# All 32 row moves of both routed layers issued one behind another, ahead of the first put

## The chip, the cores and the metric

One core of one Trainium2 chip. The metric is the time of one execution on the device in microseconds. The kernel runs a whole small network in one launch.

## The reference

Four blocks of cross-attention and feed-forward on x (4 x 512 tokens, 128 features), each with a layer norm before it and a residual add. Blocks 1 and 4 have a routed feed-forward ("layer 0" and "layer 1" in this text): each token goes to the two best of eight experts, and its results are summed with the gates. Cut to that:

```
x = x + xattn0(ln(x), ctx)
x = x + ffn0(ln(x))     # gates = softmax(x @ gate_w); top 2 of 8 experts; gelu(x @ fc[e]) @ proj[e]
x = x + xattn1(...); x = x + ffn1(...)      # dense over experts
x = x + xattn2(...); x = x + ffn2(...)
x = x + xattn3(ln(x), ctx)
x = x + ffn3(ln(x))     # top 2 of 8; (silu(x @ wg[e]) * (x @ wu[e])) @ down[e]
```

The routed layers compute only the chosen pairs of token and expert, and so does the kernel: 2048 tokens x 2 choices = 4096 rows, sorted by expert.

## The kernel before

The 2048 tokens are 16 tiles of 128. A routed layer goes through these steps:

- DVE and PE work out for each token and choice the row that it gets in a buffer in HBM, `xw` (`slot_i`), first for tiles 0 to 7, then for tiles 8 to 15. The semaphore `routed` counts the halves.
- POOL copies rows into `xw` by 32 indirect DMAs, called **moves** (`scatter`, L678 to L684): one for each tile and choice, 128 rows of 130 numbers each. They come in seven groups: tiles 0 to 4 (10 moves), 5 (2), 6 (2), 7 (2), 8 and 9 (4), 10 and 11 (4), 12 to 15 (8), from the table `MOVED` (L37). Each group counts its landings on one of four semaphores `scattered`, so group n first waits for group n - 4.
- `xw` is then read in 39 **slots** of 128 rows, each of one expert. SP loads a slot's rows into one of four buffers `xrow` (L487), as soon as the groups that it needs have landed (`FILLED`: slots 0 to 2 need group 0, slot 3 group 1, 5 group 2, 7 group 3, 9 group 4, 13 group 5, 17 group 6).
- For slot t PE transposes the rows (L2399), ACT copies the result into `xT` (L888, semaphore `ex_xc`), and PE multiplies with the up weights (L2411: 8 matmuls of 128x128 in layer 0, 16 in layer 1), which DVE has copied to `wcur` (L1440, once the up-projection four slots earlier has freed a buffer: semaphore `ex_up`). ACT applies the activation (L893, waits on `ex_up` too), in layer 1 DVE multiplies (L1455), and PE multiplies with the down weights (L2422, 8 matmuls, semaphore `ex_dn`). ACT copies the result into one of eight buffers `Y` (L904; in layer 0 every other turn of eight goes to a second set, `attn`).
- POOL writes each slot's result to its tokens' places in HBM, `yt`, by an indirect DMA, called a **put** (`put`, L686 to L700), once ACT has made it. SP loads `yt` back by pieces and DVE adds it to X.

All engines run their own program in the order written, and meet by semaphores. What sets the order of moves and puts on POOL is its function `experts(layer)` (L706 to L735) alone. Three things in it matter here:

- `BURSTS` (L38): in layer 0 groups 1, 4 and 6 wait until the group before them has landed; in layer 1 group 1 does.
- `pause()` (L702 to L704): a memset of 128x192 numbers that POOL itself then waits for. The buffer is used by nothing at that time. It stands behind each of the first 24 puts of both layers, and in layer 1 also ahead of each move from group 3 on.
- In layer 1 group 3 also waits for ACT's first copy of the layer (`ex_xc`), and the eight moves of the last group stand between the first four puts, two behind each.

Of the kernel before, what the change touches and what calls it, by code (L numbers as in the profile page):

```python
# [20 lines left out]
TILES = B * S // P  # L21
# [4 lines left out]
E, TOPK = 8, 2  # L26
# [7 lines left out]
SLOTS = (TILES * P * TOPK + PARTIAL) // P  # L34


MOVED = (0, 5, 6, 7, 8, 10, 12, TILES)  # L37
BURSTS = ((1, 4, 6), (1,))  # L38
FILLED = [-(-(tiles * P * TOPK - PARTIAL) // P) for tiles in MOVED[1:-1]]

FIRST_DONE = (GT * P * TOPK * 3 // 2 + PARTIAL) // P
# [7 lines left out]
RING = 4  # L49
# [72 lines left out]
def build(nc, p0, p1, p3, cols, rows, bias, x, mask0, mask3, fc0, pj0, fc1, pj1, fc3, pj3,  # L122
          wkv, wq2, wout2, w1t, w2t, cw, out):
    ctx = ExitStack()
    with ctx:
# [3 lines left out]
        def sem(name):  # L129
            return ctx.enter_context(nc.semaphore(name))  # L130
# [189 lines left out]
        with nc.sbuf_tensor("XHL", [P, GROUPS, 2, 2, S], F32R) as XHL:  # L320
# [55 lines left out]
        scattered = [sem(f"scattered{i}") for i in range(4)]  # L376
        table_ready, table_mm = (sem(n) for n in ("table_ready", "table_mm"))
        x_loaded = [sem(f"x_loaded{i}") for i in range(RING)]
        ex_t, ex_xc, ex_w, ex_up, ex_act, ex_dn, ex_y = (
            sem(n) for n in ("ex_t", "ex_xc", "ex_w", "ex_up", "ex_act", "ex_dn", "ex_y"))  # L380
# [47 lines left out]
        def landed(layer, group):  # L428

            def moves(groups):  # L430
                return sum(TOPK * (MOVED[i + 1] - MOVED[i]) for i in groups if i % RING == group % RING)
            return 16 * (layer * moves(range(len(MOVED) - 1)) + moves(range(group + 1)))
# [149 lines left out]
        def _(pool):  # L582
            n = [0]

            def link(ins):

                n[0] += 1
                ins.then_inc(pool_chain, 1)
                pool.wait_ge(pool_chain, n[0])
# [88 lines left out]
            def scatter(layer, group, tile, choice):  # L678

                pool.wait_ge(const_ready, 3)  # L680
                pool.wait_ge(routed, GROUPS * layer + (2 if tile >= GT else 1))
                pool.indirect_dma_start(  # L682
                    out=xw_dram, out_offset=bass.IndirectOffsetOnAxis(ap=slot_i[:, choice, tile:tile + 1], axis=0),
                    in_=XW[:, tile, :], in_offset=None).then_inc(scattered[group % RING], 16)  # L684

            def put(layer, t):  # L686

                s = t % YRING
                pool.wait_ge(dest_ready, layer * SLOTS + t + 1)
                pool.wait_ge(ex_y, layer * SLOTS + t + 1)  # L690
                if t >= RING:

                    r = (t - RING) % YRING
                    pool.wait_ge(y_put[r], 16 * (layer * uses(SLOTS, r, YRING) + uses(t - RING + 1, r, YRING)))
                if t == 0 and layer:

                    pool.wait_ge(half_done, GROUPS * layer)
                pool.indirect_dma_start(  # L698
                    out=yt_dram, out_offset=bass.IndirectOffsetOnAxis(ap=dest_i[:, t:t + 1], axis=0),
                    in_=y_slot(layer, t), in_offset=None).then_inc(y_put[s], 16)  # L700

            def pause():  # L702

                link(pool.memset(mfill[:, 0:2 * PAUSE].bitcast(F32), 0.0))  # L704

            def experts(layer):  # L706

                if layer == 0:
                    pool.wait_ge(pads_out, 16 * ((E * TILES + SPARE) // RING))
                pool.wait_ge(routed, GROUPS * layer + 1)  # L710
                last = len(MOVED) - 2
                for tile in range(MOVED[1]):
                    for choice in range(TOPK):
                        scatter(layer, 0, tile, choice)
                for group in range(1, last + (layer == 0)):
                    if group in BURSTS[layer]:
                        pool.wait_ge(scattered[(group - 1) % RING], landed(layer, group - 1))
                    if group >= RING:
                        pool.wait_ge(scattered[group % RING], landed(layer, group - RING))
                    if layer and group == RING - 1:  # L720
                        pool.wait_ge(ex_xc, SLOTS + 1)
                    for tile in range(MOVED[group], MOVED[group + 1]):
                        for choice in range(TOPK):
                            if layer and group >= RING - 1:
                                pause()
                            scatter(layer, group, tile, choice)
                pool.wait_ge(scattered[last % RING], landed(layer, last - RING))
                for t in range(SLOTS):
                    put(layer, t)
                    if layer and t < TILES - MOVED[last]:  # L730
                        for choice in range(TOPK):
                            pause()
                            scatter(layer, last, MOVED[last] + t, choice)
                    if t < PACED:
                        pause()  # L735

# [19 lines left out]
            pool.sem_inc(const_ready, 1)  # L756
            first_half_norm(0)
            experts(0)

            pool.wait_ge(in_dense, 16 * 2 * E)  # L760
# [29 lines left out]
            conv_norm()  # L790
            first_half_norm(1)
            experts(1)


# [1727 lines left out]
```

## Time and profile before

| | us |
|---|---|
| runs, lowest, median and highest of three | 608.09, 612.33, 612.35 |
| profiled execution, its own time | 611.6 |
| span of its trace | 609.5 |
| mean granted TensorE clock in it | 0.932 |

The span goes from the first to the last instruction on the core; the other 2.1 us lie around it. The moves of layer 0 run from 74.83 to 120.55 us of the span and its experts from 96 to 192 us; the moves of layer 1 run from 468.49 us on and its experts from 488 to 598 us. All stage times below are counted from the span's start. PE is the TensorE, with PEld as its weight loads, ACT the ScalarE, DVE the VectorE, POOL the GpSimd, SP the SyncE.

### The profile page before, as it was taken

What the parts mean: (1) busy time and instruction counts of PE and PEld (TensorE: products, weight loads), DVE (VectorE), ACT (ScalarE), POOL (GpSimd) and SP (SyncE); (2) the same over time, 40 slices, a digit from 0 to 9 for tenths busy, and PEclk for the clock granted to TensorE, in tenths of its full rate; (3) what the DMA queues carried; (4) which work ended last, traced back from release to release, by engine and by line L of the source; (5) the groups of instructions that cost most, each with busy time, mean ns of one, the idle gap of its engine ahead of it and who ended that gap; (6) DMA issues with size and microseconds to landing.
All of it is one profiled execution on the core that took longest, in us unless ns stands there. A gap on an engine that the chain in (4) does not pass through costs nothing.

```text
span 609.5 us, 12293 instructions
## 1 busy us (share of the span) xinstructions
PE 550.2 (90%) x3808; PEld 464.0 (76%) x3809; DVE 408.1 (67%) x1452; ACT 240.2 (39%) x551; POOL 269.1 (44%) x489
## 2 busy tenths in 40 slices
PE   4999988389999899999999978999999799999992
PEld 3577757289998499888987856766786299999992
DVE  8888873133437885475678868877887765655573
ACT  2555613135554343444442223454551043333330
POOL 3365266656656405930000010444534778874332
PEclk9999868689999889999998989998999599999997
DMA  9999013112243400000000360002200122222234
GB/s 310 379 315 269 2 49 80 57 53 71 70 136 92 120 1 1 2 1 1 1 2 0 103 175 1 2 1 70 70 1 10 57 72 64 69 57 57 78 108 120
DMA packets 48151, 47.64 MB, mean 78 GB/s; under 512 B 6470, under 2 KB 37603, under 8 KB 47942
## 3 DMA queue, kind: packets, MB, share of 16 engines
q1 hardware_dynamic: 43558, 37.68, 21.1%
q0 software_dynamic: 4544, 9.38, 4.7%
q8 instruction: 22, 0.36, 0.2%
q14 instruction: 27, 0.22, 0.1%
HBM read 27.53 MB, written 19.51 MB: 77 GB/s over the span
## 4 chain that ended last, share of the span: by engine, by line
PE 72%; DVE 19%; another core or an unknown queue 3%; issue 3%; ACT 1%; DMA 1%; DVEq 0%; POOL 0%; POOLq 0%; SPq 0%; ACTq 0%
PE bank L2411 16%; PE bank L2422 10%; PE bank L1988 8%; PE bank L2184 4%; PE bank L2229 4%; PE bank L2268 4%; PE bank L2257 2%; PE bank L1977 2%; PE bank L1978 2%; PE bank L1979 2%; PE bank L1868 2%; PE bank L2399 1%; DVE stats L1106 1%; DVE X L1510 1%
## 5 line engine op out<-in xcount | busy, mean ns | idle before, releaser
L2411 PE MATMUL bank<-xT,wcur 128*128 128x128 f32 x936 | 122.1, 282 | 13.4 <-ACT xT L888 7.5
L2411 PEld LDWEIGHTS bank<-xT,wcur 128*128 128x128 f32 x936 | 114.7, 198 | 15.7 <-issue 12.3
L641 POOL TENSOR_SCALAR var_eps<-mv 128x4 f32<-128x4 f32 (+2 forms) x12 | 2.9, 238 | 186.0 <-DVEq L1814 95.7
L698 POOL DMA_INDIRECT yt<-Y,dest_i x62 | 60.9, 983 | 53.6 <-ACT Y L904 29.1
L682 POOL DMA_INDIRECT xw<-XW,slot_i x64 | 63.4, 991 | 30.1 <-issue 15.5
L1440 DVE COPY wcur<-WA 128x512 f32 x78 | 37.7, 485 | 56.9 <-PE bank L2411 34.0
L972 ACT ACTIVATE hT<-bank,b_cols 128x512 f32<-128x512 f32 x64 | 44.0, 688 | 63.3 <-PE bank L1979 62.8
L1988 PE MATMUL bank<-WC,hT 128*128 128x128 f32 x512 | 63.8, 279 | 0.0
L1988 PEld LDWEIGHTS bank<-WC,hT 128*128 128x128 f32 x512 | 61.4, 194 | 1.4
L1584 DVE SCALAR_TENSOR_TENSOR X<-bank,G,X 128x128 f32<-128x128 f32 x128 | 36.0, 344 | 32.3 <-PE bank L1988 27.0
L1455 DVE TENSOR_TENSOR hT<-gb,bank 128x512 f32<-128x512 f32 x39 | 26.8, 688 | 40.2 <-ACT gb L893 37.6
L893 ACT ACTIVATE gb<-bank 128x512 f32<-128x512 f32 x39 | 23.3, 597 | 53.3 <-PE bank L2411 41.1
L2422 PE MATMUL bank<-WA,hT 128*128 x312 | 43.2, 285 | 0.0
L2422 PE MATMUL bank<-WB,hT 128*128 x312 | 40.9, 275 | 0.0
L2422 PEld LDWEIGHTS bank<-WA,hT 128*128 128x128 f32 x312 | 40.2, 202 | 0.0
L2422 PEld LDWEIGHTS bank<-WB,hT 128*128 128x128 f32 x312 | 37.8, 192 | 0.0
L2229 PE MATMUL bank<-M,XT 128*128 128x512 f32 x64 | 35.7, 641 | 0.0
L893 ACT ACTIVATE hT<-bank 128x512 f32<-128x512 f32 x39 | 23.3, 598 | 30.4 <-PE bank L2411 19.3
L1237 DVE TENSOR_REDUCE smax<-bank 128x16 f32<-128x512 f32 x32 | 22.0, 688 | 15.6 <-PE bank L2233 8.3
L2268 PE MATMUL bank<-VB,YT 128*128 128x36 f32 x256 | 31.9, 271 | 0.0
L2268 PEld LDWEIGHTS bank<-VB,YT 128*128 128x128 f32 x256 | 31.1, 192 | 0.3
L819 ACT ACTIVATE YT<-YT 128x512 f32<-128x512 f32 x32 | 20.2, 631 | 25.6 <-DVE YT L1238 25.5
(404 smaller groups left out, 1191.5 us busy)
## 6 DMA issues: line engine op xcount, KB each, us to landing
xw<-pad_rows SPq DMA_DIRECT2D x34, 260.0 KB, 4.1
xrow<-xw SPq DMA_DIRECT2D x78, 65.0 KB
WA<-in_fc_dram SPq DMA_DIRECT2D x16, 256.0 KB, 4.2
YT<-yt SPq DMA_DIRECT2D x16, 256.0 KB, 3.2
WA<-in_pj_dram SPq DMA_DIRECT2D x8, 256.0 KB, 5.8
WB<-in_fc_dram SPq DMA_DIRECT2D x8, 256.0 KB, 4.7
WB<-in_pj_dram SPq DMA_DIRECT2D x8, 256.0 KB, 6.1
X<-in_x_dram SPq DMA_DIRECT2D x2, 512.0 KB, 4.2
```

The costliest lines, as they stand in the source:

```text
L682: pool.indirect_dma_start(out=xw_dram, out_offset=bass.IndirectOffsetOnAxis(ap=slot_i[:, choice, tile:tile + 1], axis=0), in_=XW[:, tile, ...
L698: pool.indirect_dma_start(out=yt_dram, out_offset=bass.IndirectOffsetOnAxis(ap=dest_i[:, t:t + 1], axis=0), in_=y_slot(layer, t), in_offse ...
L893: act.activation(dst[:, 0:nc_f, :], bank[s % 2][:, 0:f].rearrange("p (c t) -> p c t", c=nc_f), L["act"]).then_inc(ex_act, 1)
L972: act.activation(hT[F1C * (u % 2) + c][:, :, :], four(bank[F1C * (u % 2) + c]), ACT.Relu, bias=b1_cols[:, F1C * e + c:F1C * e + c + 1]).th ...
L1440: ins = dve.tensor_copy(wcur[:, t % RING, i * width:(i + 1) * width], w[:, bass.ds(e, 1), :].rearrange("p a f -> p (a f)"))
L1455: dve.tensor_tensor(hT[s][:, :, :], gb[:, s % 2, :, :], bank[2 + s % 2][:, :].rearrange("p (c t) -> p c t", c=4), ALU.mult).then_inc(ex_mu ...
L1584: dve.scalar_tensor_tensor(out=X[:, t, :], in0=bank[4 + u % 2][:, j * D:(j + 1) * D], scalar=G[:, t, e:e + 1], in1=X[:, t, :], op0=ALU.mul ...
L1988: ins = pe.matmul(bank[4 + u % 2][:, j * D:(j + 1) * D], hT[F1C * (u % 2) + c][:, j, :], DOWN1[:, e, c * D:(c + 1) * D], start=(c == 0), s ...
L2229: pe.matmul(bank[s % 2][:, :], XT[:, s, :], M[:, b, :], start=True, stop=False)
L2268: ins = pe.matmul(bank[4 + j % 2][:, c * VW:(c + 1) * VW], PT[:, j % 2, c, :], VB[:, b, c, :], start=True, stop=True)
L2411: ins = pe.matmul(dst, wcur[:, s4, at:at + P], xT[s4 % 2][:, :], start=True, stop=True)
L2422: ins = pe.matmul(y, hT[s4][:, c, :], dn[:, bass.ds(e, 1), c * P:(c + 1) * P].rearrange("p a d -> p (a d)"), start=(c == 0), stop=(c == nc ...
```

## The change

POOL's `experts(layer)` issues all 32 moves of a layer first and then the 39 puts. The waits of `BURSTS`, the wait for ACT's first copy, the memsets ahead of moves and the placing of the last group between puts are gone. The waits for the group four before remain, and so do the memsets behind the first 24 puts. Nothing else differs, apart from the wait for `scattered` in front of the puts, which the group's own wait now covers.

```diff
-BURSTS = ((1, 4, 6), (1,))
...
-                for group in range(1, last + (layer == 0)):
-                    if group in BURSTS[layer]:
-                        pool.wait_ge(scattered[(group - 1) % RING], landed(layer, group - 1))
+                for group in range(1, last + 1):
                     if group >= RING:
                         pool.wait_ge(scattered[group % RING], landed(layer, group - RING))
-                    if layer and group == RING - 1:
-                        pool.wait_ge(ex_xc, SLOTS + 1)
                     for tile in range(MOVED[group], MOVED[group + 1]):
                         for choice in range(TOPK):
-                            if layer and group >= RING - 1:
-                                pause()
                             scatter(layer, group, tile, choice)
-                pool.wait_ge(scattered[last % RING], landed(layer, last - RING))
                 for t in range(SLOTS):
                     put(layer, t)
-                    if layer and t < TILES - MOVED[last]:
-                        for choice in range(TOPK):
-                            pause()
-                            scatter(layer, last, MOVED[last] + t, choice)
                     if t < PACED:
                         pause()
```

On POOL in layer 0, the 32 moves before the change, with the semaphores that each waits for (`x9` stands for nine alike):

```order
L682 DMA xw<-XW,slot_i 17408x130 [waits pool_chain,const_ready,routed,pads_out]
L682 DMA xw<-XW,slot_i 17408x130 [waits routed,const_ready] x9
L682 DMA xw<-XW,slot_i 17408x130 [waits routed,const_ready,scattered0]
L682 DMA xw<-XW,slot_i 17408x130 [waits routed,const_ready] x5
L682 DMA xw<-XW,slot_i 17408x130 [waits const_ready,routed,scattered0,scattered3]
L682 DMA xw<-XW,slot_i 17408x130 [waits routed,const_ready] x3
L682 DMA xw<-XW,slot_i 17408x130 [waits routed,const_ready,scattered1]
L682 DMA xw<-XW,slot_i 17408x130 [waits routed,const_ready] x3
L682 DMA xw<-XW,slot_i 17408x130 [waits const_ready,routed,scattered2,scattered1]
L682 DMA xw<-XW,slot_i 17408x130 [waits routed,const_ready] x7
L698 DMA yt<-Y,dest_i 12800x128 [waits ex_y,dest_ready,scattered2]
```

and after it (the lines are numbered one lower):

```order
L681 DMA xw<-XW,slot_i 17408x130 [waits pool_chain,const_ready,routed,pads_out]
L681 DMA xw<-XW,slot_i 17408x130 [waits routed,const_ready] x15
L681 DMA xw<-XW,slot_i 17408x130 [waits routed,const_ready,scattered0]
L681 DMA xw<-XW,slot_i 17408x130 [waits routed,const_ready] x3
L681 DMA xw<-XW,slot_i 17408x130 [waits routed,const_ready,scattered1]
L681 DMA xw<-XW,slot_i 17408x130 [waits routed,const_ready] x3
L681 DMA xw<-XW,slot_i 17408x130 [waits routed,const_ready,scattered2]
L681 DMA xw<-XW,slot_i 17408x130 [waits routed,const_ready] x7
L697 DMA yt<-Y,dest_i 12800x128 [waits ex_y,dest_ready]
```

The order of the moves is the same; moves 11, 17 and 25 no longer wait for the group just ahead (in the first listing `scattered0`, `scattered3` and the last `scattered1`).

On POOL in layer 1, from the 11th move to the second put before the change, with the twenty like rows in the middle left out:

```order
L682 DMA xw<-XW,slot_i 17408x130 [waits routed,const_ready,scattered0]
L682 DMA xw<-XW,slot_i 17408x130 [waits routed,const_ready] x3
L704 MEMSET mfill 128x192 [waits ex_xc]
L682 DMA xw<-XW,slot_i 17408x130 [waits routed,const_ready,pool_chain]
L704 MEMSET mfill 128x192
...
L698 DMA yt<-Y,dest_i 12800x128 [waits ex_y,half_done,dest_ready,scattered2]
L704 MEMSET mfill 128x192
L682 DMA xw<-XW,slot_i 17408x130 [waits routed,const_ready,pool_chain]
L704 MEMSET mfill 128x192
L682 DMA xw<-XW,slot_i 17408x130 [waits routed,const_ready,pool_chain]
L704 MEMSET mfill 128x192
L698 DMA yt<-Y,dest_i 12800x128 [waits ex_y,dest_ready,pool_chain]
```

and the layer's moves and first puts after it:

```order
L681 DMA xw<-XW,slot_i 17408x130 [waits pool_chain,routed,const_ready]
L681 DMA xw<-XW,slot_i 17408x130 [waits routed,const_ready] x15
L681 DMA xw<-XW,slot_i 17408x130 [waits routed,const_ready,scattered0]
L681 DMA xw<-XW,slot_i 17408x130 [waits routed,const_ready] x3
L681 DMA xw<-XW,slot_i 17408x130 [waits routed,const_ready,scattered1]
L681 DMA xw<-XW,slot_i 17408x130 [waits routed,const_ready] x3
L681 DMA xw<-XW,slot_i 17408x130 [waits routed,const_ready,scattered2]
L681 DMA xw<-XW,slot_i 17408x130 [waits routed,const_ready] x7
L697 DMA yt<-Y,dest_i 12800x128 [waits half_done,ex_y,dest_ready]
L703 MEMSET mfill 128x192
L697 DMA yt<-Y,dest_i 12800x128 [waits ex_y,dest_ready,pool_chain]
```

Moves 15 to 24 have lost their memsets, moves 25 to 32 have gone from behind puts 0 to 3 to ahead of put 0.

## Rows read from the trace of the kernel before

**Rows 1.** The page, busy time and share of the span of each engine.
```profile
PE 550.2 (90%) x3808; PEld 464.0 (76%) x3809; DVE 408.1 (67%) x1452; ACT 240.2 (39%) x551; POOL 269.1 (44%) x489
```

**Rows 2.** Busy time by stretch: from:to, length, engines' busy us, clock, DMA.
```profile
core 0: us, PE busy (x) PEld busy (x) DVE busy (x) ACT busy (x) POOL busy (x), PEclk, DMA share, GB/s
...
99.00:111.00 12.00, 7.58 (x58) 6.96 (x56) 4.05 (x20) 2.52 (x7) 7.93 (x9) 0.93 0.23 62
111.00:127.50 16.50, 7.57 (x34) 6.93 (x34) 1.45 (x7) 2.49 (x9) 11.14 (x14) 0.60 0.17 53
...
488.00:513.00 25.00, 24.85 (x216) 24.25 (x215) 16.17 (x48) 10.16 (x27) 19.46 (x29) 0.97 0.25 69
```

**Rows 3.** Groups of instructions from 131 to 169 us: DVE's weight copies.
```profile
L1440 DVE COPY wcur<-WA 128x512 f32 x20 | 11.1, 557 | 23.8 <-PE bank L2411 23.8
```

**Rows 4.** The chain of waits in order of time, from 100 to 133 us: start, length, what.
```profile
104.56 4.71 another core or an unknown queue
```

**Rows 5.** Timeline of layer 0's experts: start, length, engine, line, what [idle before].
```profile
102.18 1.06 PE L2411 MATMUL bank<-xT,wcur 128*128 128x128 f32 x8
...
109.30 0.60 ACT L893 ACTIVATE hT<-bank 128x512 f32<-128x512 f32 x1 [4.74 <-remote]
109.75 0.43 DVE L1440 COPY wcur<-WA 128x512 f32 x1 [5.60 <-remote]
...
112.69 2.07 PE L2411 MATMUL bank<-xT,wcur 128*128 128x128 f32 x8 [5.28 <-issue]
...
113.69 0.60 ACT L893 ACTIVATE hT<-bank 128x512 f32<-128x512 f32 x1 [1.05 <-remote]
114.14 0.43 DVE L1440 COPY wcur<-WA 128x512 f32 x1 [3.51 <-remote]
...
126.50 0.60 ACT L893 ACTIVATE hT<-bank 128x512 f32<-128x512 f32 x1 [5.28 <-remote]
126.94 0.43 DVE L1440 COPY wcur<-WA 128x512 f32 x1 [11.91 <-remote]
...
127.56 1.92 PE L2411 MATMUL bank<-xT,wcur 128*128 128x128 f32 x8 [2.64 <-ACT xT L888]
```

**Rows 6.** Timeline of POOL in layer 0: moves 11, 17, 25 and 32, put 3.
```profile
89.16 0.96 POOL L682 DMA_INDIRECT xw<-XW,slot_i  x1 [1.72 <-issue]
...
99.33 0.96 POOL L682 DMA_INDIRECT xw<-XW,slot_i  x1 [2.74 <-DMA xw<-XW,slot_i]
...
110.74 0.96 POOL L682 DMA_INDIRECT xw<-XW,slot_i  x1 [1.61 <-DMA xw<-XW,slot_i]
...
119.59 0.96 POOL L682 DMA_INDIRECT xw<-XW,slot_i  x1 [0.30 <-issue]
...
128.04 0.97 POOL L698 DMA_INDIRECT yt<-Y,dest_i  x1 [2.92 <-DVE dest_i L1448]
```

**Rows 7.** Timeline of POOL in layer 1: moves 1, 11, 14, 15, 16, put 0.
```profile
468.49 1.16 POOL L682 DMA_INDIRECT xw<-XW,slot_i  x1 [2.44 <-DVE slot_i L1343]
...
482.67 0.96 POOL L682 DMA_INDIRECT xw<-XW,slot_i  x1 [1.61 <-DMA xw<-XW,slot_i]
...
486.59 1.08 POOL L682 DMA_INDIRECT xw<-XW,slot_i  x1 [0.30 <-issue]
489.13 0.26 POOL L704 MEMSET mfill<- 128x192 f32 x1 [1.46 <-ACT xT L888]
489.89 0.97 POOL L682 DMA_INDIRECT xw<-XW,slot_i  x1 [0.49 <-POOL mfill L704]
...
491.40 0.97 POOL L682 DMA_INDIRECT xw<-XW,slot_i  x1 [0.28 <-POOL mfill L704]
...
505.50 1.08 POOL L698 DMA_INDIRECT yt<-Y,dest_i  x1 [0.30 <-issue]
```

**Rows 8.** Timeline of PE in layer 1: up-projections of slots 1, 5 and 6.
```profile
491.32 1.95 PE L2411 MATMUL bank<-xT,wcur 128*128 128x128 f32 x16
...
501.58 1.95 PE L2411 MATMUL bank<-xT,wcur 128*128 128x128 f32 x16
...
504.37 1.95 PE L2411 MATMUL bank<-xT,wcur 128*128 128x128 f32 x16
```

## The prediction

> **What bounds the kernel now.** I read the page first, then the stage table, the chain of waits, and the timelines of PE, ACT, DVE and POOL in the two expert stages. The page says PE is busy for 550.2 of 609.5 us while POOL is busy for 269.1 [rows 1]: POOL's own time costs nothing by itself, and only what it does to PE counts. The stage table [rows 2] shows where PE is not full. In the first 25 us of the second routed layer's experts (layer 1, 488 to 513 us) it is busy for 24.85 us; but in the first routed layer (layer 0) it is busy for 7.58 of 12.00 us from 99 to 111, and for 7.57 of 16.50 us from 111 to 127.5, at a granted clock of 0.60. Behind that the experts run smoothly there too: 20 weight copies, one a slot, in the 38 us from 131 to 169, 1.9 us a slot [rows 3]. So the one large hole next to the edited code lies in layer 0, from about 102 to 127.5 us, and layer 1 has none.
>
> What that hole is, the chain of waits tells [rows 4]: its first piece, 4.71 us long, is put down to "another core or an unknown queue", and four more like it follow up to 126.5 us. One core runs here, so the profile simply doesn't find the releaser. The timeline finds it [rows 5]. PE runs the eight up-projection matmuls of slot 3 at 102.18, and they are over at 103.24; ACT, which needs them, runs only at 109.30, and DVE, which needs the same semaphore for its next weight copy, at 109.75. The next pairs are 113.69 and 114.14, then 126.50 and 126.94: always 0.44 or 0.45 us apart. Two engines with different programs don't resume together three times unless one signal frees both, and the only signal that both wait for is PE's. So PE does its matmuls on time and its semaphore updates reach the others 6 us and more late. Meanwhile PE runs dry, because its next matmul needs what ACT and DVE make.
>
> What happens on POOL at that time [rows 6]: it issues moves one behind another, 1.27 us from start to start (0.96 us of work and 0.30 us of issue), from 99.33 to 109.1 and from 110.74 to 120.55, then three puts; the backlog is gone at 126.50, when POOL has stood still for over a microsecond (its next put is at 128.04, after 2.92 us idle). In layer 1 the same moves run beside the experts with a memset between them, so that one starts every 1.51 us (489.89, 491.40) [rows 7], and there PE keeps 2.79 us a slot (501.58 to 504.37) [rows 8]. My reading: PE's signals lag when POOL issues DMAs with no break beside the experts.
>
> **What the change does, part by part.** The sum is made against the profiled execution's own time, 611.6 us (span 609.5 us and 2.1 us around it); the median of the runs shown is 612.33, 0.7 us more.
>
> 1. Three landing waits in layer 0 go. Before moves 11, 17 and 25 POOL idles 1.72, 2.74 and 1.61 us where a step without a wait has 0.30 [rows 6]: 1.42 + 2.44 + 1.31 = 5.2 us. So the last move starts at 119.59 - 5.2 = 114.4 us. What remains in front of the moves are the waits for the group four before; its last move was issued at least 8 us earlier, and a landing takes less than the 2.74 us that these waits lasted at most, so they cost nothing. Move 17 needs the second half's slot numbers and comes at about 95 us now; DVE writes them ahead of the weight copies for slot 0, and slot 0 runs near 102.18 - 3 x 1.9 = 96.5, so they are there.
>
> 2. In layer 1 one landing wait goes (1.61 - 0.30 = 1.3 us), the wait for the first copy (489.13 - 487.67, 1.46 us) [rows 7], and 18 memsets between moves. 32 moves at 1.27 us from 468.49 end at 468.49 + 31 x 1.27 + 0.96 = 508.8 us; the first put, now at 505.50, moves to 509.1, while the later ones come sooner, having no moves between them. Put 0 frees the buffer of result 8, which PE comes to near 501.58 + 6 x 2.79 = 518 us, so the later first put holds nobody.
>
> 3. The wait's and memsets' own time is worth nothing: POOL is not on the chain, PE has no hole in layer 1, and its start there (slot 1 at 491.32) follows from the routing, the row loads and ACT's first copy, not from moves after the first ten. So layer 1 can't gain. It can lose, and that is the main term.
>
> 4. The cover that goes: in layer 1 the experts now start while POOL is 20 us into an unbroken run of moves, and it goes on for another 20 us. The nearest row for that is layer 0's hole. There PE needed from 102.18 (slot 3) to 127.56 (slot 7) for four slots, 6.35 us a slot against 1.9 [rows 3, 5]; and the backlog cleared 126.50 - 120.55 = 5.95 us after the last move, the next matmul 1.06 us later. Carried over: the last move ends at 508.8, so the backlog is gone at about 514.8 and PE is at full rate from 515.9; from slot 1 at 491.32 to then it does (515.9 - 491.3) / 6.35 = 3.9 slots, so it starts slot 5 there. Now slot 5 starts at 501.58 [rows 8]: 14.3 us lost. Then the clock: after its hole PE was granted half its clock (1.2 of 2.4 GHz), and the eight matmuls of slot 7 took 1.92 instead of 1.06 us [rows 5]; one slot of 24 matmuls at that rate is 3 x 0.86 = 2.6 us more. Against this fewer puts stand ready at the end of the moves than the three of layer 0, some two fewer, 1.5 us each: -3.0. Together +13.9 us. Bounds: from 0 (the paused steps of 1.51 us did no harm, and 1.27 is only 0.24 less) to 22 us (no signal passes before the last move ends: slot 2 starts at 512 instead of 501.58 - 3 x 2.79 = 493.2, 18.8 us, and 2.6 for the clock, rounded up).
>
> 5. Layer 0. The backlog clears 5.2 us earlier, at 121.3, and PE goes on at 122.4. But the breaks of 1.4 and 2.4 us, up to 89.16 and 99.33 us, go too, and slots 1 and 2 ran smoothly behind the second. If the slow rate holds from slot 1 on (98.4, two slots of 1.9 before 102.18), PE is at slot 1 + 24.0 / 6.35 = 4.8. At full rate slot 5 would have to start at 127.56 - 2 x 1.9 = 123.8 to be level with before. Level or 1.4 us ahead at slot 5, 0.5 behind at slot 4: I take 0, with -5.2 (same backlog, only sooner) and +4 (two slots fewer) as ends.
>
> Sum: 611.6 + 0 + 13.9 = 625.5 us.
>
> A smaller thing: DVE's weight copies (four pairs, for the first four slots) are made while the moves around 486.59 run, and that one took 1.08 us instead of the 0.96 of the one at 482.67 [rows 7]. Some moves of the unpaused run meet such copies; with all 16 that fall into the expert stage the run would end 16 x 0.12 = 1.9 us later. I leave it in the range. The Trainium skill ("SBUF — State Buffer", section "SBUF: two separate sides") has this as a trap: a DVE fp32 copy within SBUF locks GpSimd out of the shared port, so that it can't write its descriptors. By that rule alone the change would be harmless for PE, since it is POOL that waits. The trace agrees only in size, 0.12 us a move.
>
> **The rivals.**
>
> B, the only faster one: the hole in layer 0 belongs to layer 0 (to code run for the first time, say), and only its end follows the last put or move. Then layer 1 is untouched, and layer 0 ends 5.2 us sooner: 611.6 - 5.2 = 606.4. For it: in layer 1 moves beside experts did no harm at 1.51 us a step, and the three puts from 120.86 had memsets behind them too without freeing anything. Against it: ACT and DVE resume together, and their own missing instructions would not free both at once. It decides if layer 1's slots stay at 2.79 us. The Trainium skill ("Runtime: NRT & Kernel Launch", section "Instruction fetch mechanics") says that an engine refills its instruction memory in blocks by a DMA queue of its own, mostly hidden; by that rule a late block, not a late signal, would be the cause, and the change would bring what B says. No row here ties a stretch of the hole to such a block.
>
> C, the two effects are small or cancel: the lags in layer 1 cost some 2 us at the unbroken pace, and layer 0 gains as much. 611.6. For it: 0.24 us a step is little. Against it: the three long idle times removed were the only breaks that layer 0 had, and it had a hole in spite of them.
>
> D, total blocking: with no break at all no signal of PE passes until the moves end, in both layers. Layer 1: +22 as above. Layer 0: only slot 1 starts at about 118, which at 1.9 us a slot is level with 127.56 - 6 x 1.9 = 116.2: +2. Sum 635.6. For it: the lag grew during the run in layer 0, from 103.24 to 109.30 (6.1 us) for slot 3 to 114.76 to 126.50 (11.7 us) for slot 5 [rows 5]. Against it: a signal did pass in the middle of a run, at 113.69.
>
> **How the numbers follow.** A 0.50 (625.5, own range 617 to 631), D 0.17, C 0.18, B 0.15. The range for 8 in 10 reaches from 607 (C whole and B's upper side) to 637 (D's centre and a little more). A measurement of this kernel tells about 1% (6.1 us) from no change: its three runs lie 4.3 us apart. Faster by over 1% means under 606.2: a bit more than half of B, 0.09. Within 1% (to 618.5): rest of B, C and the lower edge of A, 0.25. Slower: 0.66.
>
> **What would show it.** Right, if in the changed profile layer 1 has a PE hole between 490 and 516 us with waits of unknown release in its chain, ACT and DVE resuming in pairs, and a granted clock near 0.6 there; if POOL's last move starts near 114 and 508 us; and if from about 520 us slots are at 2.79 us again. Wrong, if PE's slots in layer 1 stay at 2.79 us from the first on, or if layer 0's hole stays as long with the moves over at 115 us, since then moves don't set its end.

## The result, and the profile after

The changed kernel takes 635.41 us (median of 4 runs, 633.13 to 636.93) where the kernel before takes 610.97 (4 runs, 608.09 to 612.35): ratio 1.041, 95% interval 1.0365 to 1.0455. It is slower, by 24.4 us. Its profiled execution took 633.13 us, with a span of 631.0 us against 609.5, so 21.5 us of the loss can be read in the two traces.

PE's line of the page [rows 1] is the whole summary: a little less busy time, a longer span. The work is the same, the gaps are new.

```profile
PE 545.0 (86%) x3808; PEld 461.5 (73%) x3809; DVE 404.7 (64%) x1452; ACT 240.4 (38%) x551; POOL 260.2 (41%) x471
```

The busy time by stretch, in the three stretches of [rows 2]:

```profile
core 0: us, PE busy (x) PEld busy (x) DVE busy (x) ACT busy (x) POOL busy (x), PEclk, DMA share, GB/s
99.00:111.00 12.00, 0.00 (x0) 0.00 (x0) 0.00 (x0) 0.39 (x1) 9.11 (x10) 0.50 0.19 61
111.00:127.50 16.50, 9.43 (x57) 9.07 (x58) 5.11 (x26) 5.78 (x17) 4.37 (x6) 0.60 0.10 30
488.00:513.00 25.00, 12.47 (x71) 8.57 (x71) 6.29 (x24) 2.60 (x5) 17.05 (x18) 0.77 0.23 63
```

From 99 to 111 us PE does nothing at all (7.58 us before), and from 488 to 513 us it works for half of the time (24.85 of 25 before). Past both holes everything is as it was: 21 weight copies in the stretch of [rows 3].

```profile
L1428 DVE COPY wcur<-WA 128x512 f32 x21 | 11.5, 548 | 22.6 <-PE bank L2399 22.5
```

The chain of waits (start, length, what) has one long piece in each layer, where [rows 4] had shorter ones, the first of 4.71 us. First layer 0, then layer 1:

```profile
93.60 0.08 PE bank L1895
93.67 23.46 issue
117.14 1.23 PE bank L2387 x2
```

```profile
483.05 0.37 PE bank L2338 x2
483.42 8.88 issue
492.30 4.26 PE bank L1856 x10
```

"issue" is time for which the profile finds no releaser. The timelines find it. Layer 0, which answers to [rows 5, 6], PE, ACT and POOL in turn (start, length, engine, line, what, idle before):

```profile
93.01 0.59 PE L1893 MATMUL bank<-row,ones_row 1*128 1x8 f32 x2
...
117.14 0.66 PE L2387 MATMUL bank<-ident,xrow 128*128 128x128 f32 x2 [23.46 <-issue]
118.72 2.07 PE L2399 MATMUL bank<-xT,wcur 128*128 128x128 f32 x8 [0.93 <-ACT xT L876]
...
93.86 0.60 ACT L860 ACTIVATE M<-bank 128x512 f32<-128x512 f32 x1 [9.66 <-remote]
98.79 0.60 ACT L860 ACTIVATE M<-bank 128x512 f32<-128x512 f32 x1 [4.33 <-issue]
116.29 0.28 ACT L853 ACTIVATE M<-bank 128x128 f32<-128x128 f32 x1 [16.90 <-remote]
...
113.03 0.96 POOL L681 DMA_INDIRECT xw<-XW,slot_i  x1 [0.31 <-issue]
114.29 0.96 POOL L681 DMA_INDIRECT xw<-XW,slot_i  x1 [0.30 <-issue]
126.47 0.98 POOL L697 DMA_INDIRECT yt<-Y,dest_i  x1 [11.21 <-DVE dest_i L1436]
```

PE had done its last matmuls for ACT at 93.7 us; ACT's next instruction that needs them starts at 116.29, 1.04 us after POOL's last move has ended (114.29 + 0.96 = 115.25). PE waits for ACT. So the signal was held for over 20 us, and slot 0's up-projection starts at 118.72 instead of 96.55. The hold grew during the run of moves: of the same engine's copies of `M` just before, the one at 93.86 comes 3.2 us and the one at 98.79 6.4 us later than in the kernel before (90.68 and 92.38).

Layer 1, which answers to [rows 7, 8]: POOL, PE, DVE, ACT.

```profile
489.55 0.96 POOL L681 DMA_INDIRECT xw<-XW,slot_i  x1 [0.30 <-issue]
493.30 1.15 POOL L681 DMA_INDIRECT xw<-XW,slot_i  x1 [2.78 <-DVE slot_i L1331]
...
512.66 0.96 POOL L681 DMA_INDIRECT xw<-XW,slot_i  x1 [0.30 <-issue]
517.81 1.03 POOL L697 DMA_INDIRECT yt<-Y,dest_i  x1 [4.19 <-issue]
...
482.98 0.44 PE L2338 MATMUL bank<-entries,ones_f 39*128 39x78 f32 x2
...
497.04 2.05 PE L2399 MATMUL bank<-xT,wcur 128*128 128x128 f32 x16
...
508.37 0.37 PE L2410 MATMUL bank<-WB,hT 128*128 x1 [1.13 <-issue]
...
514.76 3.75 PE L2399 MATMUL bank<-xT,wcur 128*128 128x128 f32 x16 [5.91 <-issue]
...
522.98 1.95 PE L2399 MATMUL bank<-xT,wcur 128*128 128x128 f32 x16
...
491.76 0.20 DVE L1390 COPY eid_f<-bank 128x39 f32<-128x39 f32 x1 [8.19 <-remote]
...
513.29 0.60 ACT L881 ACTIVATE gb<-bank 128x512 f32<-128x512 f32 x1 [11.96 <-remote]
```

There are two holes here. PE finishes the table that says which expert each slot belongs to at 483.42, and DVE copies it only at 491.76, 1.25 us after POOL's 16th move has ended and POOL stands still for 2.78 us. Without the table no weights are copied, and slot 0 starts at 497.04 instead of 489.12. Then POOL goes on without a break. Slot 1's matmuls were over at 501.0 (499.04 + 1.95), and ACT, which takes their result, gets to it at 513.29, after 11.96 us, 0.33 us before the last move ends. Slot 5 starts at 522.98; before, at 501.58.

### The profile page after: what moved, and what is told of

It reads as the page before. It is cut to its first block, busy times and chain, and to the rows that moved or that the text cites. A ratio compares the mean times of both kernels' runs of the same rounds, so it can differ in the third digit from the quotient of the medians.

```text
span 631.0 us, 12272 instructions
## 1 busy us (share of the span) xinstructions
PE 545.0 (86%) x3808; PEld 461.5 (73%) x3809; DVE 404.7 (64%) x1452; ACT 240.4 (38%) x551; POOL 260.2 (41%) x471
## 4 chain that ended last, share of the span: by engine, by line
PE 72%; DVE 18%; issue 8%; DMA 1%; ACT 1%; DVEq 0%; POOL 0%; SPq 0%; POOLq 0%; ACTq 0%
PE bank L2399 17%; PE bank L2410 10%; PE bank L1976 8%; PE bank L2172 4%; PE bank L2217 4%; PE bank L2256 4%; PE bank L2245 2%; PE bank L1965 2%; PE bank L1966 2%; PE bank L1967 2%; PE bank L1856 1%; PE bank L2387 1%; DVE stats L1094 1%; PE bank L2314 1%; PE bank L2207 1%
## 5 line engine op out<-in xcount | busy, mean ns | idle before, releaser
L1428 DVE COPY wcur<-WA 128x512 f32 x78 | 35.9, 461 | 38.5 <-PE bank L2399 36.4
L2410 PE MATMUL bank<-WB,hT 128*128 x312 | 42.5, 279 | 3.0 <-issue 3.0
L2387 PE MATMUL bank<-ident,xrow 128*128 128x128 f32 x78 | 21.8, 282 | 23.6 <-issue 23.5
L2410 PE MATMUL bank<-WA,hT 128*128 x312 | 40.9, 275 | 0.0
L2410 PEld LDWEIGHTS bank<-WA,hT 128*128 128x128 f32 x312 | 37.8, 192 | 0.0
L1436 DVE TENSOR_SCALAR dest_i<-xrow,eid_f 128x1 int32<-128x1 f32 x78 | 20.6, 264 | 26.7 <-PE bank L2387 25.4
```

What stands on the lines that cost most here:

```text
L1428: ins = dve.tensor_copy(wcur[:, t % RING, i * width:(i + 1) * width], w[:, bass.ds(e, 1), :].rearrange("p a f -> p (a f)"))
L2387: pe.transpose(bank[4 + s4 % 2][:, 0:P], xrow[s4][:, 0:D], ident[:, :]).then_inc(ex_t, 1)
L2410: ins = pe.matmul(y, hT[s4][:, c, :], dn[:, bass.ds(e, 1), c * P:(c + 1) * P].rearrange("p a d -> p (a d)"), start=(c == 0), stop=(c == nc ...
```

## The experiments

The runs came in four sets (runs 1 to 4, 5 to 8, 9 and 10, 11 and 12), each from one chip, on three chips in all. On two of these (the first, the third and the fourth set) the kernel before takes 610 to 617 us by its medians, as in the first measurement, and on the third (the second set) 586.55 us. All ratios are to runs of the kernel before on the same chip. They stand with their 95% intervals and are not the quotients of the two medians, from which they differ by up to 0.4%. The runs are called the first to the twelfth, in the order in which they stand here. "Slot n" is the start of slot n's up-projection on PE. Theory S: PE's semaphore updates are held while POOL issues indirect DMAs with no long enough break. The edits are written here as lines of the kernels before and after; the runs made the same ones by a table of switches.

### One layer at a time

Layer 0 as changed, layer 1 as before, which is one line of the kernel before:

```diff
-BURSTS = ((1, 4, 6), (1,))
+BURSTS = ((), (1,))
```

> The change in layer 0 alone. From the changed kernel's profile (its layer 1 starts 1.9 us later than before, and the whole is 21.5 us longer in span): theory S (PE's signals are held while POOL issues moves without a break; the loss stands in the layer where the run overlaps work) gives +2 us, 613 us, and PE idle from about 94 to 117 us again. If the two layers' losses hang together (a later start of layer 1 pushing it into something else), it would be +8 or more.

Measured: 1.0045 (1.0008 to 1.0083), 620.69 against 616.32 us. PE is idle from 94.3 to 119.5 us. A hole of 25 us costs next to nothing, since the kernel before has one there that costs almost as much.

The reverse, the changed kernel with layer 0's landing waits put back:

```diff
+                    if group in ((1, 4, 6), ())[layer]:
+                        pool.wait_ge(scattered[(group - 1) % RING], landed(layer, group - 1))
```

> The change in layer 1 alone. Theory S: about +20 us (21.5 less the 1.9 of layer 0), 631 us, with the copy of the slot table on DVE some 8 us late and PE's full rate only behind the last move. If the loss needs layer 0's change as well, under +10.

Measured: 1.0253 (1.0199 to 1.0308), 634.07 us. Slot 0 of layer 1 starts at 498.42 and slot 5 at 525.33. So most of the loss is layer 1's. The two parts' ratios come to 3.0% together, while both at once cost 4.1% in the first measurement and 4.6% in the ninth run; the rest of about 1% stays open.

### Memsets alone, and waits with memsets

The changed kernel with a memset ahead of each move from the 11th on:

```diff
                         for choice in range(TOPK):
+                            if group >= 1: pause()
                             scatter(layer, group, tile, choice)
```

> The changed kernel with nothing but a memset ahead of each move from the 11th on, in both layers (no landing waits, no wait for the first copy, all moves ahead of the first put). Theory S (the break is what counts, 0.25 us more between two moves): layer 1 loses at most 3 us, and layer 0's hole of about 20 us mostly goes, so 595 to 606 us. Rival L (what lets signals through is the drained queue, that is the landing waits and the wait for the first copy; memsets are incidental): holes in both layers stay, 625 us or more.

Measured: 1.0053 (1.0022 to 1.0084), 620.09 us: neither range. In layer 1 the stutter is gone, with 2.79 us a slot from slot 2 up to about 517 us. The late start stays, slot 0 26.2 us after the layer's first move (491.24 - 465.00; in the kernel before 489.12 - 468.49 = 20.6), and layer 0 keeps a hole, now in two pieces:

```profile
103.03 0.66 PE L2400 MATMUL bank<-ident,xrow 128*128 128x128 f32 x2 [8.80 <-issue]
...
115.26 2.08 PE L2412 MATMUL bank<-xT,wcur 128*128 128x128 f32 x8 [3.38 <-issue]
```

Then layer 0 was handled exactly as the kernel before handles layer 1:

```diff
-BURSTS = ((1, 4, 6), (1,))
+BURSTS = ((1,), (1,))
-                    if layer and group == RING - 1:
-                        pool.wait_ge(ex_xc, SLOTS + 1)
+                    if group == RING - 1:
+                        pool.wait_ge(ex_xc, layer * SLOTS + 1)
-                            if layer and group >= RING - 1:
+                            if group >= RING - 1:
...
-                    if layer and t < TILES - MOVED[last]:
+                    if t < TILES - MOVED[last]:
```

> The kernel before with layer 0's moves in the manner of layer 1: one landing wait, a wait for the first copy, a memset ahead of each move from the 15th on, the last eight moves behind the first four puts. Theory S: the hole from 102 to 127 us goes for the most part; it costs 18 us against full rate, of which some 10 to 16 come back: 595 to 601 us. Rival C (cold code or something else of layer 0 makes the hole): it stays, 610 us or somewhat more, since the last moves come later.

Measured: 0.9959 (0.9921 to 0.9997), 615.18 us against 616.32: between the two expectations, nearer to the rival's. The hole of 25 us is gone, but from 107 us on a slot takes 3.8 us and more, because each signal is still late by some 2 us, and layer 0's slots have only 1.9 us of work to cover that where layer 1's have 2.79:

```profile
110.93 1.15 PE L2412 MATMUL bank<-xT,wcur 128*128 128x128 f32 x8 [1.65 <-issue]
111.92 1.06 PE L2423 MATMUL bank<-WA,hT 128*128 x8
112.81 0.27 PE L2400 MATMUL bank<-ident,xrow 128*128 128x128 f32 x1
114.75 1.15 PE L2412 MATMUL bank<-xT,wcur 128*128 128x128 f32 x8 [1.66 <-ACT xT L889]
```

### Is it POOL being busy, or POOL issuing DMAs?

In layer 1, far from the moves, six memsets of 128x1024 stand back to back ahead of put 23, and puts 29 to 34 are held until result 34 is there and then go without a break.

```diff
+                    if layer and t == 23:
+                        pool.wait_ge(ex_y, layer * SLOTS + t + 1)
+                        for _ in range(6):
+                            link(pool.memset(mfill[:, :].bitcast(F32), 0.0))
+                    if layer and t == 29:
+                        pool.wait_ge(ex_y, layer * SLOTS + t + 6)
                     put(layer, t)
```

> The kernel before; in layer 1, ahead of put 23, POOL runs six memsets of 128x1024 back to back (each an estimated 1.1 to 1.3 us from the 0.27 us of one of 128x192), and puts 29 to 34 are held until result 34 is there and then issued directly one behind another (six at 1.26 us, 7.6 us). Theory S (POOL's back-to-back issue of indirect DMAs holds PE's signals): nothing happens at the memsets, PE keeps 2.79 us a slot there; at the six puts ACT and DVE stand still for some microseconds while PE's matmuls of the slot are over, and PE has a hole of 3 to 6 us; in all +3 to +6 us. Rival P (any unbroken work of POOL holds them, by the shared port or its sequencer): a hole of the same kind at the memsets too, +6 to +12 us. Rival M (only moves do it, since they read the rows in SBUF): no hole at either, within 1 us.

Measured: 592.25 us in one run against 586.55, and no hole at either place. This chip is the one that needs 586.55 us, and the trace shows why: nothing is held there at all. The next kernel of this set of runs has the changed kernel's layer 0, with all 32 moves in a row from 74.41 to 115.24 us and the first put at 115.54, and this beside them:

```profile
98.00:120.00 22.00, 22.00 (x198) 22.00 (x198) 11.62 (x47) 12.39 (x36) 17.18 (x20) 0.99 0.32 84
```

PE is busy for 22.00 of 22.00 us. So the kernels of this set say nothing about what a break does on a chip that holds signals; they say that where nothing is held no break is needed.

The changed kernel with one wait back, the one for ACT's first copy:

```diff
+                    if layer and group == RING - 1:
+                        pool.wait_ge(ex_xc, SLOTS + 1)
```

> The changed kernel with one wait back: in layer 1 POOL waits ahead of the eleventh move group's start (move 15) for ACT's first copy, without memsets. The late table signal (slot 0 at 497 instead of 489 us) should be gone and the stutter behind it stay, since the 18 moves left still go without a break. If both parts count for themselves: layer 1 loses some 11 to 14 us instead of 19.5, so 6 to 8 us less than the changed kernel, ratio to before about 1.02. If the stutter alone sets the end (rival: the backlog clears only when the moves end, and these now end no sooner): no less than the changed kernel, ratio about 1.03 to 1.04. If one break of some microseconds cures layer 1 as the memsets do: ratio about 1.005.

Measured: 0.9982 (0.9951 to 1.0014), 585.24 us; layer 1's slots keep 2.79 us with 18 unbroken moves beside them.

The fourth kernel with small memsets in layer 0, between moves and behind puts:

```diff
-                                pause()
+                                pause(PAUSE if layer else 4)
```

> The fourth kernel (layer 0 handled as layer 1), but all memsets of layer 0, between moves and behind puts, write 4 columns instead of 192, an estimated 0.1 us instead of 0.27. If it is the existence of a break of another instruction between two issues that lets PE's signals pass (theory B): no hole in layer 0, POOL's steps shorter by 0.15 us, and the time 0 to 6 us under the fourth kernel's, ratio to before 0.985 to 0.996. If the length of the break counts (theory L): PE holes of several microseconds return between 100 and 130 us, and the ratio is 1.000 to 1.010.

Measured: 1.0105 (1.0069 to 1.014), 593.59 us. The loss is no held signal but rows that come late: one PE wait of 5.85 us for `xrow` ends at 129.74. With the first-copy wait and the last eight moves behind puts, layer 0's moves are over at 126.10 us here, and at 119.27 in the eighth run, which has neither in layer 0.

The kernel before with small memsets between layer 1's moves:

```diff
-                                pause()
+                                pause(4)
```

> The kernel before with the memsets between layer 1's moves cut to 4 columns; nothing else. Theory B (a break's existence counts): within 0.3% of before, slots in layer 1 at 2.79 us. Theory L (its length counts): lags of PE's signals of several microseconds between 490 and 516 us, +4 to +12 us, ratio 1.007 to 1.02.

Measured: 0.9988 (0.9961 to 1.0015), 586.26 us.

None of the four runs could decide between its theories, since this chip holds nothing. Hence the next set took the changed kernel along.

> The changed kernel itself, word for word, since the runs with the first-copy wait and with tiny memsets came from a chip on which the kernel before takes 586 us and layer 0 has no hole at all. Theory S now says: PE's signals are held back on some chips only. If this chip is one with the hole (before at 608 to 617 us), the ratio is 1.03 to 1.045; if it is one without (before near 586), nothing is held back, and the change gives at most the waits: ratio 0.995 to 1.005. Rival T (the hole belongs to what the other chip happened to have in step, and a longer unbroken run brings it out anywhere): 1.03 to 1.045 on either.

Measured: 1.0463 (1.0423 to 1.0504), 638.53 against 610.44 us. The chip holds signals, and the result is repeated. Rival T is answered by the sixth run: on the other kind of chip the longest run of moves there is, all 32 of layer 0, brought no hole. Whether the change costs nothing on the other kind of chip was not measured with the changed kernel itself; the kernel with the one wait stands for it.

> The changed kernel with layer 1's first-copy wait back ahead of move 15 (no memsets between moves), and late in layer 1 six memsets of 128x1024 back to back ahead of put 23 (6.9 us) and puts 29 to 34 held and then issued directly one behind another. On a chip with the hole: the table's signal comes in time (slot 0 near 491 instead of 497 us), the stutter of the 18 moves behind it stays, and layer 1's early part loses 8 to 14 us instead of 19.5; nothing happens at the six memsets (rival: any unbroken work of POOL holds the signals, then PE has a hole of 3 to 6 us there); at the six puts ACT and DVE stand still for microseconds. Ratio 1.02 to 1.04. On a chip without the hole: PE runs through all of it, and what is left is some 4 to 6 us for the held puts (as in the run with two bursts), ratio 1.005 to 1.012.

Measured: 1.0498 (1.0453 to 1.0543), 642.14 us, above the expected 1.02 to 1.04. Four readings, first the early part of layer 1 (POOL, PE):

```profile
487.00 0.96 POOL L683 DMA_INDIRECT xw<-XW,slot_i  x1 [0.30 <-issue]
496.10 0.96 POOL L683 DMA_INDIRECT xw<-XW,slot_i  x1 [8.14 <-ACT xT L896]
...
495.88 2.05 PE L2419 MATMUL bank<-xT,wcur 128*128 128x128 f32 x16 [0.15 <-ACT xT L896]
...
511.75 0.37 PE L2419 MATMUL bank<-xT,wcur 128*128 128x128 f32 x1 [0.33 <-issue]
513.17 0.59 PE L2419 MATMUL bank<-xT,wcur 128*128 128x128 f32 x2 [1.04 <-issue]
514.58 0.37 PE L2419 MATMUL bank<-xT,wcur 128*128 128x128 f32 x1 [0.83 <-issue]
```

The wait brings the start forward by little: slot 0 comes 25.5 us after the first move (495.88 - 470.35) instead of 26.6 in the changed kernel's first trace and 28.3 in its second. The reason can be read: POOL first issues 14 moves without a stop, up to 487.96, and DVE gets the table only at 490.33, 7.1 us after PE has finished it. And the 18 moves behind the wait, over at 518.90, cost more than in the changed kernel: slot 5 starts 31.8 us after slot 0 (527.63 - 495.88), there 25.9 and 26.2. From the first move to slot 5 it is 57.3 us, against 52.6 and 54.6. So the wait alone gives nothing back, and the rival with the stutter as the end of all was right.

Then the two bursts (POOL's memsets; ACT and PE at the held puts, which POOL issues, with one more behind them, from 618.05 to 626.72):

```profile
586.75 6.92 POOL L734 MEMSET mfill<- 128x1024 f32 x6 [0.82 <-ACT Y L912]
...
623.04 0.60 ACT L901 ACTIVATE gb<-bank 128x512 f32<-128x512 f32 x1 [2.95 <-remote]
626.69 0.28 ACT L912 ACTIVATE Y<-bank 128x128 f32<-128x128 f32 x1 [3.05 <-issue]
...
627.23 2.07 PE L2430 MATMUL bank<-WB,hT 128*128 x8 [3.93 <-issue]
```

Beside the memsets PE has no gap, and ACT's `gb` comes 1.99 us after its matmuls began (590.98 - 588.99), as anywhere else. Beside the puts it comes 3.48 us after them (623.04 - 619.56). On the chip that holds nothing, the same instruction in the same place:

```profile
570.72 1.95 PE L2419 MATMUL bank<-xT,wcur 128*128 128x128 f32 x16
...
572.71 0.60 ACT L901 ACTIVATE gb<-bank 128x512 f32<-128x512 f32 x1 [1.45 <-PE bank L2419]
```

Again 1.99 us. So puts hold PE's signals as moves do, and a POOL that is busy without issuing DMAs does not. The bursts don't part the issuing on POOL from the transfers that follow it: a move lands some 1.6 us after its issue is over (481.06 to 482.67 in [rows 7], the landing wait), and the signals come free from 0.3 us before to 3.2 us after the last issue ends. Which of the two holds them, no run tested.

### Does a break count by being there or by its length?

The kernel before, with layer 1's memsets at 4 columns (0.12 us instead of 0.27) and the same two bursts:

> The kernel before with the memsets between layer 1's moves cut to 4 columns, and late in layer 1 six memsets of 128x1024 back to back ahead of put 23 and puts 29 to 34 held and then issued directly one behind another. The held puts cost 4 to 8 us on either kind of chip. On a chip with the hole (before at 608 to 617 us): if the existence of a break lets PE's signals pass (theory B), slots of layer 1 keep 2.79 us and slot 5 starts near 501.6 us as before, ratio 1.007 to 1.014; if its length counts (theory L), lags of microseconds at 490 to 516 us, slot 5 at 505 us or later, ratio 1.015 to 1.035. At the six memsets nothing on any chip. On a chip without the hole: ratio 1.007 to 1.014 and no lag anywhere.

Measured: 1.0247 (1.0179 to 1.0314), 633.15 against 616.80 us, on a chip that holds signals. POOL, ACT and PE in layer 1:

```profile
490.12 0.12 POOL L705 MEMSET mfill<- 128x4 f32 x1
490.51 0.97 POOL L683 DMA_INDIRECT xw<-XW,slot_i  x1 [0.28 <-POOL mfill L705]
491.48 0.12 POOL L705 MEMSET mfill<- 128x4 f32 x1
...
500.85 0.60 ACT L901 ACTIVATE gb<-bank 128x512 f32<-128x512 f32 x1 [6.30 <-remote]
...
504.31 3.79 PE L2419 MATMUL bank<-xT,wcur 128*128 128x128 f32 x16 [1.50 <-ACT xT L896]
...
523.94 3.78 PE L2419 MATMUL bank<-xT,wcur 128*128 128x128 f32 x16 [0.18 <-DVE hT L1463]
```

Slot 5 starts 20.9 us after slot 0 (12.5 in the kernel before), slot 8 35.6 us after it (20.8). Between the end of a move and the start of the next lie 0.30 us without a memset, 0.39 with the small one, 0.55 with the full one. The first two delay signals beside the experts by 5 us and more (in this run slot 2's `gb`, due near 494.3, comes at 500.85), the third by some 2. The length counts, not the presence of another instruction; whether it is the gap or the number of issues in a given time can't be told, since a longer gap changes both. But the third clears nothing that has piled up in an unbroken run ahead of it: in the third kernel the memsets of layer 1 stood from move 11 on, and DVE still got the table at 486.61, 6.8 us after PE had finished it (1.4 in the kernel before), just as POOL's 16th move ended and POOL stood still. Stops of POOL are what clears such a backlog in these traces. The held puts did the same as in the run before, with a PE wait of 5.42 us behind them.

> The kernel of the seventh run again (layer 0 handled as layer 1, all its memsets cut to 4 columns), since that run came from a chip without the hole, where it was 1% slower than before by a wait for rows of 5.85 us. On a chip with the hole: theory B (a break's existence counts) no lag of PE's signals beyond that of the fourth kernel, which had 0.27 us memsets and a slot each 3.8 us from 107 to 131 us, and a time at or below it, ratio 0.985 to 0.997; theory L (its length counts) longer holes than there, ratio 1.000 to 1.015.

Measured: 1.000 (0.9952 to 1.0049), 615.53 us. The holes are longer than in the fourth kernel, 3.04 us at 110.86 and 6.86 us at 121.10, as theory L (the break's length counts) says. No kernel of the study clearly beats the kernel before on its chip: the fourth comes nearest, 0.4% below it by an interval that almost touches 1.

## Why the prediction was right in its kind, and which step missed

Forecast: 625.5 us, range 607 to 637, slower with 0.66. Measured: 635.41, slower. That is inside the range and near its upper end; the likeliest value missed by 9.9 us. Rival D (total blocking, given 0.17) said +2 and +22 and 635.6. Its sum agrees to 0.2 us, but that is partly luck: the traces show +1.9 and +19.5, the medians lie 24.4 us apart where the traces lie 21.5 apart, and layer 1 went otherwise: D keeps slots 0 and 1 on time and holds slot 2, while in the trace slot 0 was 7.9 us late and slot 3 was the one held.

**The mechanism** was read rightly. [Rows 5] showed ACT and DVE resuming together behind a late signal of PE, and the two runs with bursts on chips that hold signals show that POOL's indirect DMAs cause it and its memsets don't. Rival B (a hole of layer 0's own, code run for the first time) is out: on the chip that holds nothing, the same code has PE busy for 22.00 of 22.00 us.

**Steps 1 and 2, POOL's times.** The last move of layer 0 started at 114.29, forecast 114.4. In layer 1 the moves were over at 513.6, forecast 508.8: 1.9 us because the layer began later, and 2.5 for a wait that the step didn't have (2.78 instead of 0.30), for the second half's slot numbers. It belongs to the same cause, since DVE makes them behind the table copy that was late.

**Step 5, layer 0.** Forecast 0, ends -5.2 and +4; the layer 1 behind it began 1.9 us later (470.41 against 468.49), and layer 0 changed alone costs 0.45%, about 2.8 us. The size was near, the course was not. The step carried over 6.35 us a slot from slot 1 on; in truth slot 0 itself waited until 118.72, because the held signals were those of PE's work ahead of the experts, which ACT copies before slot 0 can start (98.79, then 116.29). The loss was moved, from between slots 3 and 7 to ahead of slot 0.

**Step 4, the main term.** Forecast +13.9, measured +19.5 (slot 5: 522.98 - 501.58 = 21.4, less the 1.9 carried in). From slot 0 to slot 5 it now takes 522.98 - 497.04 = 25.9 us instead of 12.5: 13.5 us lost there. That is the forecast's 14.3 + 2.6 - 3.0 within half a microsecond, and luck in part: the step had 6.35 us a slot and the backlog gone 5.95 us after the last move, while three slots went through at once, the next was held for 12.7 us (502.03 to 514.76), and the signal came 0.33 us before the last move ended, itself 4.8 us later than forecast. What is missing is 6.0 us ahead of slot 0: 26.6 us from the first move to slot 0 instead of 20.6.

**So the step that failed** is a sentence of step 3: that layer 1's start "follows from the routing, the row loads and ACT's first copy, not from moves after the first ten". The table is made by PE (483.42) in the middle of moves 1 to 16 (470.41 to 490.51), so its signal is subject to the same lag. The argument was applied to the experts and not to what comes ahead of them. What had protected it was the landing wait ahead of move 11, priced at its 1.3 us of POOL time:

| | with the landing wait | without it |
|---|---|---|
| from layer 1's first move to slot 0, us: chips that hold signals | 20.6 (before), 21.5 (eleventh run), 22.2 (fourth), 22.3 (twelfth), 22.7 (first) | 25.5 (tenth), 26.2 (third), 26.6 (changed), 28.3 (ninth), 28.6 (second) |
| the chip that holds nothing | 17.8 (fifth), 18.2 (seventh), 18.8 (eighth) | 18.5 (sixth) |
| from the end of PE's table to DVE's copy of it, us: chips that hold signals | 1.0 (first), 1.3 (twelfth), 1.4 (before), 1.5 (fourth), 2.0 (eleventh) | 6.5 (second), 6.8 (third), 7.1 (tenth), 8.3 (changed), 8.8 (ninth) |
| the chip that holds nothing | 0.1 (eighth), 0.4 (fifth, seventh) | 0.4 (sixth) |

(All kernels of the left column also have the wait for the first copy and memsets ahead of moves. The tenth run has that wait without the landing wait and the third the memsets without it, and neither replaces it; no run has the landing wait alone.)

**The rest of the range.** "-3.0 for fewer puts" and "+2.6 for the clock" can't be told apart here. The granted clock did fall after the hole: it was 0.64 from 513 to 523 us, and slot 3's 16 matmuls took 3.75 us instead of 1.95. From 490 to 516 us it was 0.76, where the prediction's sign said near 0.6.

The Trainium skill ("SBUF — State Buffer", section "SBUF: two separate sides") has a copy of DVE keep GpSimd from writing its descriptors, and by that rule POOL is the one that waits. The trace agrees, by 0.12 us (the move at 494.75, beside such copies, took 1.08 us instead of 0.96). The runs show an effect in the other direction that is larger by far: POOL's issues delay what PE tells the others.

## What to carry to other kernels

Where POOL issues indirect DMAs in a row, look at the start of the instructions that wait for PE, not at PE: if ACT and DVE resume together, "remote", at a stop of POOL (up to 3.2 us behind its last issue in these runs), the signal was held. Leave a real gap between issues wherever some engine waits for PE, 0.55 us between the end of one and the start of the next here, and more where a slot has little work to hide a late signal; a token break of 0.39 us did not do here. And price a wait that a change removes by all that could happen while it lasted, also for work of another kind beside it, not by the engine's own time.

## What the runs showed of the hardware that was not expected

- **Chips differ in this.** The same kernel before takes 586.55 us on one chip and 610 to 617 us on the two others, by its medians. With the tiny memsets, the first move of layer 1 starts at 448.44 us on the one and at 466.85 on the other. The 18.4 us between them arise in the hole of [rows 5]: layer 0's slot 8 already starts at 107.30 on the one and at 128.87 on the other. Why one chip holds nothing stays open: the runs show no difference in POOL's own rows, 0.96 us an issue and 0.30 between two.
- **Held signals stop PE itself.** Late in a hold PE's matmuls come singly, 1.4 us apart (511.75, 513.17, 514.58 in the tenth run), near POOL's 1.27 us from issue to issue. That each issue lets one update pass would fit; no run tested it.
- **A hold can last over 20 us** (93.7 to 116.3 in layer 0), while signals did pass in the middle of unbroken runs, at 113.69 in the kernel before [rows 5] and at 93.86 and 98.79 in the changed one. What lets one through stays open.
